# Weighted sums in pairs, reciprocals turned in the query bank, and another order of folds and output weights in the front of a cross-attention and filter kernel

## What is computed

```python
q = layernorm(x) @ wq + bq            # x: 2 x 2048 x 512, 16 heads of 32
k, v = ctx @ wk + bk, ctx @ wv + bv   # ctx: 2 x 128 x 512
score = (q k^T / sqrt(32)) * mask; score = where(score == 0, -1e9, score)
x = x + (softmax(score) @ v) @ wo + bo
x = x + real(ifft(fft(layernorm(x)) @ (wr + i wi))) + bf
```

## Time and profile before

| | us |
|---|---|
| median of three runs | 472.79 (472.09 to 473.57) |
| the profiled execution | 471.82 |
| its span, first to last instruction | 470.0 |
| PE busy in the span | 449.7 |
| DVE busy | 415.9 |
| ACT busy | 373.9 |
| POOL busy | 364.5 |

### The profile page before, as it was taken

The page is one execution under the profiler, slowest core; times in us unless marked ns, Lnnn a source line. Parts: engine busy times, 40 slices in busy tenths (PEclk is TensorE's granted clock), DMA queues, the critical chain, the costliest instruction groups (busy, mean ns, idle before and its releaser), DMA issues.

```text
span 470.0 us, 11312 instructions
## 1 busy us (share of the span) xinstructions
PE 449.7 (96%) x3538; PEld 297.8 (63%) x3538; DVE 415.9 (88%) x698; ACT 373.9 (80%) x1431; POOL 364.5 (78%) x519
## 2 busy tenths in 40 slices
PE   6989879898999999999999999999999999999997
PEld 5777557677566666666666666666666666555543
DVE  3797799999999898989999999989898999999552
ACT  3359559789998889899898988898988898899720
POOL 6589657897989979787979797987979882868562
PEclk9999989999999999999999999999999999999999
DMA  8999902332444554444544545353632432341143
GB/s 284 395 352 294 270 11 67 86 86 68 94 105 117 115 135 114 128 120 119 140 108 113 131 102 158 85 137 103 128 78 71 90 82 74 84 91 44 48 112 113
DMA packets 83308, 59.37 MB, mean 126 GB/s; under 512 B 39729, under 2 KB 70705, under 8 KB 82738
## 3 DMA queue, kind: packets, MB, share of 16 engines
q1 hardware_dynamic: 82816, 58.55, 46.2%
q10 hardware_dynamic: 434, 0.10, 0.1%
HBM read 29.27 MB, written 8.39 MB: 80 GB/s over the span
## 4 chain that ended last, share of the span: by engine, by line
PE 80%; DVE 8%; issue 4%; ACT 3%; DMA 2%; POOL 1%; SPq 0%; DVEq 0%; POOLq 0%
PE bank L396 33%; PE bank L468 16%; PE bank L522 10%; PE bank L539 7%; PE bank L401 5%; PE bank L510 5%; PE bank L535 3%; ACT zs L624 2%; DMA cxs<-in_ctx 2%; DVE zs L784 1%; DVE zs L791 1%; PE bank L471 1%; DVE nmin L796 1%; DVE lp L839 1%; POOL x L1002 1%
## 5 line engine op out<-in xcount | busy, mean ns | idle before, releaser
L624 ACT ACTIVATE zs<-zs,nbias 128x128 f32<-128x128 f32 x512 | 199.8, 397 | 19.7 <-POOL nbias L1016 19.6
L624 ACT ACTIVATION_READ_ACCUMULATOR zs<-zs,nbias 128x1 f32 x512 | 99.6, 194 | 0.0
L791 DVE SCALAR_TENSOR_TENSOR zs<-zs 128x1024 f32<-128x1024 f32 x64 | 91.8, 1435 | 2.3
L784 DVE TENSOR_TENSOR zs<-bank,ms 128x512 f32<-128x512 f32 x128 | 82.0, 682 | 0.0
L796 DVE TENSOR_REDUCE nmin<-zs 128x8 f32<-128x1024 f32 x64 | 77.2, 1206 | 0.1
L633 ACT COPY pt<-bank 128x512 f32<-128x512 f32 x128 | 67.8, 582 | 7.0 <-PE bank L522 6.8
L468 PE MATMUL bank<-xth,wqh 128*128 128x256 f16 x256 | 70.7, 276 | 2.2 <-DVE kl L743 1.8
L468 PE MATMUL bank<-xth,wql 128*128 128x256 f16 x256 | 70.2, 274 | 0.0
L468 PE MATMUL bank<-xtl,wqh 128*128 128x256 f16 x256 | 70.1, 274 | 0.0
L522 PE MATMUL bank<-ident,zs 128*128 128x128 f32 x512 | 66.9, 274 | 1.0 <-ACT zs L624 1.0
L522 PEld LDWEIGHTS bank<-ident,zs 128*128 128x128 f32 x512 | 57.4, 140 | 5.7 <-ACT zs L624 4.4
(11 more groups left out here) (109 smaller groups left out, 954.7 us busy)
## 6 DMA issues: line engine op xcount, KB each, us to landing
xs<-in_x SPq DMA_DIRECT2D x16, 512.0 KB, 4.4
xtr<-in_xt SPq DMA_DIRECT2D x16, 512.0 KB, 5.1
out<-x SPq DMA_DIRECT2D x32, 256.0 KB, 2.5
qs<-qh SPq DMA_DIRECT2D x120, 64.0 KB, 2.0
lp<-in_lparts SPq DMA_DIRECT2D x4, 1024.0 KB, 9.8
qs<-ql SPq DMA_DIRECT2D x60, 64.0 KB, 2.0
ms<-in_mask SPq DMA_DIRECT2D x16, 128.0 KB, 2.4
wqs<-in_wq SPq DMA_DIRECT2D x2, 512.0 KB, 6.4
```

Source lines behind the costliest of these rows:

```text
L624: last = act.activation(z, z, ACT.Exp, bias=nbias[:, s % 4, i:i + 1], scale=-NEG, accum_out=zsum[:, s % 4, i:i + 1])
L784: dve.tensor_tensor(zs[:, s % NZ, t], A[n % 2][:].rearrange("p (h k) -> p h k", h=4), ms[:, c % NM, t, :].unsqueeze(1).broadcast_to([128, ...
L791: dve.scalar_tensor_tensor(out=z, in0=z, scalar=0.0, in1=z, op0=ALU.is_equal, op1=ALU.subtract).then_inc(eq_done, 1)
```

## The change

`plan()` is changed so that the weighted sums of two steps stand together, ahead of `turn`, in each even step v (steps v-4 and v-3), each in its own half of CX. The `rzb` transposes move out of `weigh` into the last fill of the step, in the free right half of its bank G (`turn_rz`); where no query is left, a fill `R` is made for them alone (12 of them). The `stat_rows` transposes become a fill of their own (`ST`) ahead of the third query quarter. `copy_rec` reads the G bank and stands behind `copy_pt`; the `hi` and `lo` of the held query fills move ahead of the second half of the exponentials and ahead of `ctx_norm`. In the front: `U` and `M` one step later; folds 6 to 8 on DVE between the query fills before step 2; folds 9 to 11 on POOL at the end of step 5; the cast of the output weights on ACT in step 3, `low_o` on POOL in step 4; and another order of loads on SP.

```diff
-        4: [("U", 0)], 5: [("U", 1)], 6: [("U", 2)], 7: [("U", 3)],
-        8: [("M", 0)], 9: [("M", 1)], 10: [("M", 2)], 11: [("M", 3)],
+        5: [("U", 0)], 6: [("U", 1)], 7: [("U", 2)], 8: [("U", 3)],
+        9: [("M", 0)], 10: [("M", 1)], 11: [("M", 2)], 12: [("M", 3)],
...
-        late = [("Q",) + f for f in queries.get(v, [divmod(v + 9, 4)]) if f[0] < NC]
+        late = []
+        for f in queries.get(v, [divmod(v + 9, 4)]):
+            if f[1] == 2 and 3 <= f[0] + 1 < NC:
+                late.append(("ST", f[0] + 1))
+            if f[0] < NC:
+                late.append(("Q",) + f)
+        if 0 <= v - 3 < NS and not late:
+            late.append(("R", v - 3))
...
+        if 0 <= v - 3 < NS:
+            turned[v - 3] = len(fills) - 1
         items = []
+        if v % 2 == 0 and 0 <= v - 4 < NS:
+            items += [("PV", v - 4), ("PV", v - 3)]
...
-        if 0 <= v - 3 < NS:
-            items += [("PV", v - 3)]
...
             load_mask(1)
+            load_parts(2)
+            load_xt(3)
+            stack_k(sp)
+            stack_q(1)
             sp.wait_ge(w_lo, 2)
             sp.dma_start(wos[:], w_view(wo)).then_inc(d_wo, 16)
-            load_xt(3)
-            stack_k(sp, (lambda: load_parts(2), lambda: load_parts(3),
-                         lambda: sp.dma_start(tb[:], tables).then_inc(d_tb, 16)))
             load_x(4)
-            stack_q(1)
+            sp.dma_start(tb[:], tables).then_inc(d_tb, 16)
+            load_parts(3)
...
+            def turn_rz(o, s):
+                pe.wait_ge(p_rz, s + 1)
+                for t in range(2):
+                    last = pe.transpose(o[:, 256 + 128 * t:384 + 128 * t], rzb[:, s % 2, 4 * t:4 * t + 4, :], ident[:])
+                return last
...
-                if s >= 1:
-                    pe.wait_ge(cn_done, s)
+                if s >= 2:
+                    pe.wait_ge(cn_done, s - s % 2)
...
-                pe.wait_ge(p_rz, s + 1)
-                for t in range(2):
-                    pe.transpose(CX[:, 256 + 128 * t:384 + 128 * t],
-                                 rzb[:, s % 2, 4 * t:4 * t + 4, :], ident[:])
+                o = slice(256 * (s % 2), 256 * (s % 2) + 256)
...
             def copy_rec(s):
-                act.wait_ge(pv_done, s + 1)
-                act.copy(rec[:, s % 2, :], CX[:, 256:512]).then_inc(rc_done, 1)
+                act.wait_ge(g_done, turned[s] + 1)
+                if s >= 2:
+                    act.wait_ge(cn_done, s - 1)
+                act.copy(rec[:, s % 2, :], G[turned[s] % 3][:, 256:512]).then_inc(rc_done, 1)
...
             def ctx_norm(s):
                 dve.wait_ge(rc_done, s + 1)
+                dve.wait_ge(pv_done, s - s % 2 + 2)
...
-                if v == 3:
+                if v == 4:
                     low_o()
+                if v == 5:
+                    for n in (9, 10, 11):
+                        fold(n)
```

More of the change, by code:

```diff
@@ L34, in plan @@
 def plan():
-    fills, slots, held = [], {}, []
+    fills, slots, held, turned = [], {}, [], {}
     lead = [("W1", 0), ("CT", 0), ("CT", 1), ("K", 0), ("ST", 0), ("Q", 0, 0), ("Q", 0, 1), ("S", 0),
@@ L81, in plan @@
         held = lates
-    return fills, front, slots
+    return fills, front, slots, turned
 def stats_slot(c, t):
@@ L105, in build @@
 def build(nc, x, xt, ctx_in, mask, wq, bq, wk, bk, wv, bv, wo, bo, lparts, tables, bf, eye, sums, pick, out):
-    fills, front, slots = plan()
+    fills, front, slots, turned = plan()
     at = {f: n for n, f in enumerate(fills)}
@@ L261, in stack_head, with stack_k @@
                               src[32 * j:32 * j + 32, c % 2, :, :]).then_inc(d_q[c % 2], 16)
-        def stack_k(eng, between):
+        def stack_k(eng):
             for k in range(3):
@@ L408, in stat_rows @@
                 return last
+            step_of = {n: s for s, n in turned.items()}
+            def turn_rz(o, s):
[3 more added lines that the diff above has]
+                return last
             def fill(n):
@@ L441, in fill @@
                 elif kind == "U":
-                    pe.wait_ge(l_done if c < 2 else l_hi, 6)
+                    pe.wait_ge(l_done, 6 if c < 2 else 9)
+                    if c >= 2:
+                        pe.wait_ge(l_hi, 3)
                     pe.wait_ge(d_tb, 16)
@@ L471, in fill @@
                     last = pe.matmul(o[:, 0:256], wz[:, g], srow[:, c % 2], start=False, stop=True)
-                    if f == 2 and 3 <= c + 1 < NC:
-                        last = stat_rows(o, c + 1)
                 elif kind == "WO":
@@ L486, in fill @@
                                            for k in range(4)])
+                if n in step_of:
+                    last = turn_rz(o, step_of[n])
                 last.then_inc(g_done, 1)
@@ L688, in _ @@
                     copy_pt(v - 2, 1)
-                if v == 2:
+                if 0 <= v - 4 < NS:
+                    copy_rec(v - 4)
+                for n in held:
+                    hi(n)
+                if v == 3:
                     act.wait_ge(d_wo, 16)
@@ L697, in _ @@
                     ctx_hi(v - 4)
-                if 0 <= v - 9 < 4:
-                    high_m(v - 9)
-                for n in held + mids:
+                if 0 <= v - 10 < 4:
+                    high_m(v - 10)
+                for n in mids:
                     hi(n)
@@ L752, in lo @@
                     return
-                elif kind == "ST":
+                elif kind in ("ST", "R"):
+                    if kind == "R":
+                        dve.wait_ge(rc_done, c + 1)
                     dve.engine_nop().then_inc(g_free, 1)
@@ L907, in _ @@
             lo(at["Q", 1, 0])
+            fold(6)
             lo(at["Q", 1, 1])
+            fold(7)
             lo(at["Q", 1, 2])
+            fold(8)
             lo(at["Q", 1, 3])
@@ L918, in _ @@
                     zero_to_neg(v)
+                if 0 <= v < NS:
+                    least(v)
+                for n in held:
+                    lo(n)
                 if 0 <= v - 4 < NS:
                     ctx_norm(v - 4)
[L921 to L924, removed]
-                for n in held + mids:
+                if 0 <= v - 10 < 4:
+                    low_m(v - 10)
+                for n in mids:
                     lo(n)
@@ L940, in _ @@
                     last_lo2(r)
-                if v in (3, 4):
-                    for n in range(3 * v - 3, 3 * v):
-                        fold(n)
         @block.gpsimd
```

15 lines of the change are left out of this document (5 added, 10 removed).

## The result

The changed kernel takes 488.92 us (median of 4 runs, 488.88 to 490.68), the kernel before beside it 473.18: a ratio of 1.034, with a 95% interval from 1.031 to 1.038. Forecast were 470.8 us and a range from 466.6 to 473.6, with a chance of 0.19 for slower. The profiled execution has a span of 487.1 us, 17.1 more than the 470.0 of before.

A forecast was written before the change was run, and what follows sets the result against it. Front to about 88 us bound by waits (POOL replacing DVE), then by PE's work. From step 8: +2.4 late, +1.73 fill, -4.7 sums, -2.1 stalls, +0.6 end; 0.1 kept back, -2.0: 470.8 us, range 466.6 to 473.6.

The forecast's parts named there:

- The seam of a pair: Weighted sums on PE: one entry and exit for four passes, 1.14 us against 1.32, saving 0.18 per pair.
- This wait should not grow: PE's wait for ctx_norm ahead of a pair: norm some 1.5 us later, wanted about 1.8 later; one wait, not two.
- I count the whole gain in the long stretch: Stretch after the front: DVE, going from 94% to 95.5% busy, can follow, so the pairs' saving comes through.
- the prediction's signs: Profile after: no PE wait on cn, step 8 starting at 90 to 93 us; refuted by PE waits between 150 and 400.
- the long stretch doesn't follow: Rival, long stretch: DVE at 95.5% or the extra fill gives back half of the 4.7 us: 473.1; chance 0.15.
- changes no term: Front: POOL's three folds could hold DVE 3.75 us by contention, counted as nothing since DVE waits there for others.
- The extra fills put no work on PE and make DVE release one more bank: ST and R fills: a full-width fill then waits for earlier queries to be read, which ACT and DVE do earlier.
- two stalls of this kind, 2.1 us: Waits for ctx_norm ahead of sums, lying where DVE is fullest, should go: 2.1 us saved.
- The front: Up to step 8: POOL replaces DVE as bound, load lands at 54.4 us, step 8 later by 1.0 to 4.1, taken 2.4.
- the output weights land late: Rival, ACT's wait in step 3: load at 62.4 gives 478.8 us; over 0.3% slower if after 57.8; chance 0.12.
- The clock: Front, PE at 1.2 GHz after waiting: up to 1.8 us in both kernels, put at nothing unless in step 8 or later.

The follow-up runs named there:

- e5: Changed kernel with ctx_norm back between zero_to_neg and least on DVE, and copy_rec ahead of the held query copies on ACT: 478.13 us, ratio 1.012.
- e10: Changed kernel with norm early, output weights' load ahead of the stack_q copies, and statistics transposes in CX's free half: 468.21 us, ratio 0.990.
- e15: e10 with POOL's low_o at step 3 ahead of xtl, not at step 4: 465.19 us, ratio 0.985.
- e8: Kernel before with only the statistics transposes made a fill of their own: 477.51 us, ratio 1.0125.
- e9: e4 with the statistics transposes of chunks 4 and up in CX's free half, no fill of their own: 471.99 us, ratio 0.998.
- e4: e1 with ctx_norm back between zero_to_neg and least on DVE, and copy_rec ahead of copy_pt on ACT: 477.20 us, ratio 1.010.
- e11: Changed kernel with only the output weights' load issued ahead of the stack_q copies of chunk 1: 484.68 us, ratio 1.025.
- e6: e2 with the output weights' load issued ahead of the stack_q copies of chunk 1: 475.25 us, ratio 1.005.
- e2: Kernel before with only the changed front (loads, folds, output weights, U and M one step later), sums single: 481.68 us, ratio 1.020.
- e13: Changed kernel with only the statistics transposes of chunks 4 and up in CX's free half, norm still late: 489.04 us, ratio 1.034.
- e1: Changed kernel's loop with the front of the kernel before (folds, output weights, U and M, loads): 494.50 us, ratio 1.043.
- e16: e6 with POOL's low_o at step 3 ahead of xtl, no pairs: 472.30 us, ratio 1.000.
- e12: Changed kernel with POOL's copy of the reciprocals (rzb, spread) moved behind nbias in its step: 504.10 us, ratio 1.067.

## Why the prediction was wrong, by its own steps

**The seam of a pair: right.** The changed kernel, PE in order of time around one pair:

```profile
219.93 0.38 PE L427 MATMUL bank<-ident,rzb 128*128 128x128 f32 x2
220.24 1.07 PE L558 MATMUL bank<-pt,vs 128*32 128x256 f32 x16
221.25 1.09 PE L544 MATMUL bank<-ident,zs 128*128 128x128 f32 x8
```

Entry 0.20 behind the second transpose, 0.24 between passes, 0.31 at the exit. From the first matmul of the pair to the next instruction there are 1.01 us, and with the entry's extra 0.09 that is 1.10, where 1.14 was forecast. The row of the trace was the better guide than the rule on row groups in the Trainium skill, "TensorE: Matmul & The Clock Gate", section "The mechanism" (the prediction named the section behind it). That section also exempts a load that goes to the background weight buffer, which the prediction left out; which of the two held here no run shows. Where PE is the bound again (e5, e10, e15), a step takes 6.18 to 6.19 for 6.32, 0.13 less where 0.09 were forecast. From step 18 to 50 that is 4.1 to 4.5 us, where the forecast comes to 2.9. So the gain was put too low, not too high: the pair itself explains 0.22 of the 0.27 per two steps, and the rest stays open.

**"This wait should not grow", "I count the whole gain in the long stretch": wrong, and the largest error, 10.8 us (e5, both parts of its edit).** PE did wait for the norm, five times and 8.0 us in all, where the prediction's signs had said not at all; but that is the smaller part. I had costed the late norm by who waits for it on PE. I did not cost it on DVE, in whose order it stands. There it left a gap it had filled, made ACT's and POOL's copies late, and so shifted POOL's passes onto `zero_to_neg`. DVE's share was to go from 94% to 95.5%; it went to 97.7% (195.31 of 200), and PE had the waits between 150 and 400 us that the prediction had named as its refutation:

```profile
PE bank L490 <- DVE ql L780: 5.0, 9, 0.6
```

The rival "the long stretch doesn't follow" had the right place and DVE as the cause, but was priced at half of the gain; in fact nothing came through and the step got 0.05 longer.

The prediction did name the mechanism: the Trainium skill ("SBUF — State Buffer", section "Who interferes with whom") lets a DVE instruction with two SBUF inputs contend with POOL reading SBUF, and the runs agree, 1.22 at the least and up to 2.21 where a POOL pass was under way. But I applied it to the folds alone, and concluded that it "changes no term". It changed the one term that counted, the length of the DVE instruction that both kernels have in every step.

**"The extra fills put no work on PE and make DVE release one more bank": wrong, some 5 us (e8, e9 against e4, e10).** The bank was costed, its turn in the rotation was not. With three banks, each fill more within a step makes the next one wait for an older reader, and that reader, DVE, stands behind `least`. That the "two stalls of this kind, 2.1 us" would go did not come true either: the changed kernel still waits 1.6 us for the norm ahead of step 12's pair, and 2.3 for a bank at step 13, which DVE frees behind `least`. I also missed a loop of waits in steps 10 to 13 of the changed kernel:

```profile
DVE ml L797 <- ACT mh L620: 4.6, 4, 1.6
```

ACT's `mh` stands behind `ctx_hi`, as before, but that now waits for the late norm, and DVE waits for `mh`.

**The front: the chain was right link by link, but short.** The load landed at 55.9 (I said 54.4, and 57.8 as the point from which it decides); POOL's `low_o` ran from 72.7; `rzb` of step 2 was done at 77.2 (75.3 to 77.0); chunk 4's `split_lo` ended at 92.05 (88.4 to 91.6). What the chain left out came between these links. The pair of step 6 stands ahead of its `turn`, so step 6's `turn` began at 79.75 and not at 77.2. In step 7 PE stood 2.1 us for the bank of `ST`, until 91.39, so chunk 4's low halves were there (92.05) before PE came to the fill that reads them. And there was a wait that the chain never touched. DVE in order of time in step 5:

```profile
71.46 0.41 DVE L831 TENSOR_TENSOR cn<-bank,rec 128x256 f32<-128x256 f32 x1
76.97 0.43 DVE L749 BATCH_NORM_STATS2 stu<-bank 128x6 f32<-128x256 f32 x1 [5.10 <-POOL wol L1078]
```

DVE's part of `U` is written into the buffer of `wos`, and so waits for `low_o`: 5.10 us in which DVE, which had been full from 60 to 80, did nothing. In my count DVE only gained there. And the load cost PE a stall at the start of step 4, since exponentials stand behind ACT's wait:

```profile
61.36 1.97 PE L544 MATMUL bank<-ident,zs 128*128 128x128 f32 x8 [5.59 <-ACT zs L641]
```

I had followed ACT and POOL to step 8 and not asked what PE does meanwhile. The rival "the output weights land late" had this mechanism, but I let it begin at 57.8; it cost 4.2 us (e11) to 6.4 (e6) with the load at 55.9. Step 8's `turn` began 7.2 late; by the prediction's own count, in which the pair of step 8 is still left, step 8 began at 95.4, 6.2 late, not 2.4. e2 shows 8.9 for the front alone.

**The clock: put at nothing, and not quite nothing.** The changed kernel from 39 to 92 us has a mean granted clock of 0.87, the kernel before 0.97, e15 1.00 (the same columns as the earlier trace rows); the changed kernel first:

```profile
39.00:92.00 53.00, 40.01 (x290) 30.00 (x289) 36.66 (x59) 33.09 (x114) 34.97 (x41) 0.87 0.47 146
```

```profile
39.00:92.00 53.00, 46.57 (x382) 35.23 (x381) 45.44 (x77) 40.60 (x145) 45.43 (x56) 1.00 0.54 163
```

After its wait at step 13, 2.3 us, a query fill of the changed kernel took 2.58 us, where the earlier trace rows have 1.42; from 141 to 144 us the granted clock is 0.50:

```profile
140.53 2.58 PE bank L490 x12
```

So this fill took another 1.2 us behind the stall, at the lower level of 1.2 GHz. No run separates the cost of the clock from that of the stalls, and the parts below hold both.

**The account.** Place of the norm 10.8, load 4.2, and 5.7 left for the statistics' bank (20.7 - 10.8 - 4.2, a remainder and not a measurement of its own; e13 shows nothing for it alone): 20.7. That is the loss of 15.7 and 5.0 beyond, which fit the 4.1 to 4.5 that the shorter steps save from 18 to 50. The remaining wait behind `low_o` is worth 3.0 (e10 to e15). That the parts overlap (e1 is slower than the whole change, though it has less of it) is shown; how the overlap divides step by step is not.

## What to carry to other kernels

When an instruction is moved in an engine's program, cost three things and not one: who waits for its result, what it leaves open at its old place, and which passes of other engines are under way when the next long instruction of this one starts. Where buffers rotate, count fills and not work: an extra fill of no work still takes a turn, and the next one waits for an older reader. And a pair that is worth 0.13 us a step is seen only if the engine behind the bound, here DVE at 94%, keeps its slack; measure the loop alone and the front alone, and then the two together: here each alone, mended, gave nothing (e9, e16), and both gave 7.4 us.

## What the runs showed of the hardware

I had not expected that `zero_to_neg` (128 x 1024, two SBUF inputs) would range from 1.22 to 2.03 us within the changed kernel's stretch from 150 to 350 us, in a pattern that repeats every four steps, set by how much of a POOL pass is left when it starts; nor that POOL suffers as much, 0.40 to 1.40 us for the `rzb` copy. With mean lengths of 1.40 (e5), 1.60 (changed) and 1.94 (e12) the steps took 6.19, 6.37 and 6.62 us. The length alone does not fix the step: e13 has 1.61 and 6.29, with DVE fuller (197.27 of 200 from 200 to 400 us), and e10 1.47 and 6.18, where PE is the bound. Nor had I expected the clock to stay at full level through all of e15's profiled execution, whose page has

```profile
PEclk9999999999999999999999999999999999999999
```

though PE still waits 2.85 us at step 4 and 2.76 at step 7, while in the changed kernel it fell during or right behind waits of 5.6, 4.4 and 2.3 us. The length of a wait alone does not tell here whether the clock falls.
